# A reordered second tile list, and gathers of two sequences moved ahead of three scatters on GpSimd

## What is computed

```python
x = x + 0.5 * ffn(layernorm(x))      # 12 experts, 3 per token, hidden size 512, exact gelu
x = x + attn(layernorm(x))           # gates, convolution along the sequence, norm, gated dense layers
x = x + 0.5 * ffn(layernorm(x))
```

## Time and profile before

| what | us |
|---|---|
| median of 3 runs | 615.02 (612.63 to 616.59) |
| the profiled execution's own time | 614.01 |
| its span, first to last instruction | 612.3 |
| PE busy in it | 559.2 |
| POOL busy in it | 403.8 |

### The profile page before, as it was taken

How to read it: one execution, slowest core, us unless ns; L and a number is a source line. 1 busy time by engine, 2 the same in 40 slices (tenths; PEclk the granted TensorE clock), 3 DMA queues, 4 the chain that set the end, 5 groups by cost and what they waited for, 6 DMA issues and landing times.

```text
span 612.3 us, 17470 instructions
## 1 busy us (share of the span) xinstructions
PE 559.2 (91%) x4625; PEld 523.3 (85%) x4625; DVE 369.6 (60%) x1735; ACT 514.3 (84%) x1462; POOL 403.8 (66%) x424
## 2 busy tenths in 40 slices
PE   6899887999999999989899798998799799999996
PEld 6789887999999888868799697877699799999992
DVE  7977899441111586988775578997727632232225
ACT  4547994799989989889988699988689789989885
POOL 1076577777746777137677777767777777777771
PEclk9789999899999999999999799999999999999999
DMA  7997243243463434112355333232254532433264
GB/s 197 316 234 212 54 135 88 79 131 104 123 180 101 123 87 118 52 48 71 91 160 136 87 88 98 83 107 67 67 148 111 139 89 72 117 90 85 64 232 138
DMA packets 99127, 72.28 MB, mean 118 GB/s; under 512 B 13520, under 2 KB 91910, under 8 KB 99033
## 3 DMA queue, kind: packets, MB, share of 16 engines
q1 hardware_dynamic: 83032, 43.62, 25.7%
q0 software_dynamic: 13024, 26.11, 15.0%
q10 hardware_dynamic: 2976, 1.44, 0.8%
HBM read 37.08 MB, written 34.75 MB: 117 GB/s over the span
## 4 chain that ended last, share of the span: by engine, by line
PE 32%; DVE 21%; POOL 17%; issue 12%; ACT 8%; DMA 7%; ACTq 1%; DVEq 1%; POOLq 0%; SPq 0%
PE ps L1017 12%; PE ps L1032 12%; POOL YG L822 10%; DMA YG<-ys,SY 4%; POOL xs L806 4%; ACT hT L1205 3%; POOL yk L832 3%; DVE YG L1717 2%; DMA yk<-Ys,row 2%; PE ps L1007 2%; DVE st L1274 2%; DVE Ys L2059 1%; DVE X L1330 1%; PE ps L987 1%; DVE X L1316 1%
## 5 line engine op out<-in xcount | busy, mean ns | idle before, releaser
L1205 ACT ACTIVATE hT<-ps,BU 128x128 f32<-128x128 f32 x900 | 261.5, 392 | 43.9 <-PE ps L1017 34.5
L1017 PE MATMUL ps<-xT,WT 128*128 128x128 f32 x1800 | 243.1, 279 | 8.6 <-ACT hT L1205 5.5
L1032 PE MATMUL ps<-WD,hT 128*128 x1800 | 240.9, 277 | 6.8 <-DVE Ys L2059 6.8
L1017 PEld LDWEIGHTS ps<-xT,WT 128*128 128x128 f32 x1800 | 222.9, 194 | 18.2 <-issue 16.4
L1032 PEld LDWEIGHTS ps<-WD,hT 128*128 128x128 f32 x1800 | 221.4, 194 | 8.4 <-issue 8.3
L806 POOL DMA_INDIRECT xs<-XN,SX x144 | 142.4, 989 | 70.7 <-issue 63.3
L822 POOL DMA_INDIRECT YG<-ys,SY x132 | 130.6, 990 | 49.3 <-issue 35.4
L1088 ACT ACTIVATE WT<-WU 128x512 f32 x225 | 150.2, 668 | 7.5 <-DVE eW L1750 3.3
L2059 DVE TENSOR_TENSOR Ys<-ps,BD 128x128 f32<-128x128 f32 x225 | 54.8, 285 | 146.5 <-PE ps L1032 140.4
L832 POOL DMA_INDIRECT yk<-Ys,row x71 | 70.7, 995 | 21.9 <-issue 12.2
L793 POOL DMA_INDIRECT xl<-xna,SG x24 | 23.1, 961 | 37.4 <-DMA xna<-XN 27.6
(11 more groups left out here) (366 smaller groups left out, 592.2 us busy)
## 6 DMA issues: line engine op xcount, KB each, us to landing
ys<-Ys SPq DMA_DIRECT2D x41, 256.0 KB
xl<-xs SPq DMA_DIRECT2D x94, 64.0 KB
xl<-xs SPq DMA_DIRECT2D x71, 66.0 KB
WU<-in_L_ffn_Wup_dram SPq DMA_DIRECT2D x12, 256.0 KB, 4.6
WD<-in_L_ffn_Wdown_dram SPq DMA_DIRECT2D x12, 256.0 KB, 4.7
YG<-yk SPq DMA_DIRECT2D x4, 768.0 KB, 6.2
xs<-XN,SX POOLq DMA_INDIRECT x144
YG<-ys,SY POOLq DMA_INDIRECT x132
```

Source lines behind the costliest of these rows:

```text
L1017: x = e.matmul(HB[i % 2][:, c * P:(c + 1) * P], WT[i % NW][:, c, :], xT[m % 2][:, j * P:(j + 1) * P], start=True, stop=True)
L1032: x = e.matmul(YB[u % 2][:, j * D:(j + 1) * D], hT[i % 3][:, c * P:(c + 1) * P], WDf[:, bass.ds(r + c * P, P)], start=(c == 0), stop=(c == ...
L1205: x = e.activation(hT[i % 3][:, c * P:(c + 1) * P], HB[i % 2][:, c * P:(c + 1) * P], ACT.Gelu, bias=BU[:, bass.ds(b + c, 1)])
```

## The change

`FRONT[1]` goes from 3 to 2 and the front of list 1 from 12 to 24 tiles: these now hold every tile, begun or full, that has rows of sequences 4 and 5, filled up with other tiles of the list. Since begun tiles also hold rows of later sequences, the first load of list 1 waits for the scatters of all four sequences. POOL gathers sequences 4 and 5 after the first 24 tiles of list 1 are stored, and does so before it scatters sequences 0 to 2 for list 2.

```diff
-FRONT = (HS, 3, 2, 3)
-GA = tuple(-((E * (P - 1) - (K * (AT[1] * (n == 1) + 4 * f) - FULL * (n == 1)) * P) // P) // 4 for n, f in enumerate(FRONT))
+FRONT = (HS, 2, 2, 3)
+GA = tuple((K * (AT[1] + 4 * f) + E - FULL) // 4 if n == 1 else -((E * (P - 1) - K * 4 * f * P) // P) // 4
+           for n, f in enumerate(FRONT))
...
-POOL = (("Y", 0), ("Y", 1), ("Y", 2), ("Y", 3), ("K", 0), ("K", 1), ("K", 2), ("Y", 4), ("Y", 5), ("Y", 6), ("Y", 7),
+POOL = (("Y", 0), ("Y", 1), ("Y", 2), ("Y", 3), ("Y", 4), ("Y", 5), ("K", 0), ("K", 1), ("K", 2), ("Y", 6), ("Y", 7),
         ("K", 3), ("K", 4), ("K", 5), ("K", 6), ("K", 7))
...
                 if g == 0:
-                    for w in scattered(n, FRONT[n]):
+                    for w in scattered(n, FRONT[n] if n > 1 else len(SEQS[n])):
                         e.wait_ge(*w)
...
                 if t == 0 and k == 0:
                     e.wait_ge(s_sy, n + 1)
-                    for m in range(GROUP0[n + 1] - NYS, GROUP0[n + 1]):
+                if k == 0 and (t == 0 or n == 1 and t == 4 * FRONT[1]):
+
+                    done = GROUP0[1] + GA[1] if n == 1 and t == 0 else GROUP0[n + 1]
+                    for m in range(done - NYS, done):
                         for w in stored(m):
                             e.wait_ge(*w)
...
-                    dv.on(e.scalar_tensor_tensor(c7[:], part, -float(P - 1), c4[:], ALU.add, ALU.add))
+                    dv.on(e.tensor_tensor(c7[:], part, c4[:], ALU.add))
...
+                    dv.on(e.tensor_tensor(remX[:], nte[:], donW[:], ALU.subtract))
...
+                    dv.on(e.tensor_tensor_scan(rem[:], one[:], remX[:], 0.0, ALU.mult, ALU.add))
...
-                    dv.on(e.tensor_tensor(rem[:], endW[:], remW[:], ALU.subtract))
-                    dv.on(e.tensor_tensor(basW[:], endW[:], donW[:], ALU.subtract))
+                    dv.on(e.tensor_tensor(rem[:], rem[:], remX[:], ALU.subtract))
+                    e.wait_ge(s_dv, dv.n)
+                    dv.on(e.tensor_scalar(rem[:], rem[:], endW[:, E:EX], None, ALU.add))
                     e.wait_ge(s_dv, dv.n)
                     dv.on(e.tensor_scalar(rem[:], rem[:], -1.0, float(NTL[0] + NA[1]), ALU.mult, ALU.add))
+                    e.wait_ge(s_dv, dv.n)
+                    dv.on(e.scalar_tensor_tensor(remX[:], rem[:], 0.0, remX[:], ALU.max, ALU.min))
+                    e.wait_ge(s_dv, dv.n)
+                    dv.on(e.tensor_tensor(remW[:], remW[:], remX[:], ALU.add))
+                    dv.on(e.tensor_tensor(don4[:], donW[:], remX[:], ALU.add))
+                    e.wait_ge(s_dv, dv.n - 1)
+                    dv.on(e.tensor_tensor_scan(endW[:], one[:], remW[:], 0.0, ALU.mult, ALU.add))
+                    e.wait_ge(s_dv, dv.n)
+                    dv.on(e.tensor_scalar(endW[:], endW[:], endC[:, E:EX], None, ALU.add))
...
-                    dv.on(e.scalar_tensor_tensor(don4[:], rem[:], 0.0, remW[:], ALU.max, ALU.min))
-                    e.wait_ge(s_dv, dv.n)
-                    dv.on(e.tensor_tensor(don4[:], don4[:], donC[:], ALU.add))
-                    e.wait_ge(s_dv, dv.n)
                     dv.on(e.tensor_tensor(rem[:], nte[:], don4[:], ALU.subtract))
```

More of the change, by code:

```diff
@@ L428, in macaron_kernel @@
             "wB", "remB", "endB", "basB", "don1", "don2", "donC", "remC", "endC", "basC", "endR", "basR"))
-        donW, remW, endW, basW, don4 = (sb(n, [P, EX]) for n in ("donW", "remW", "endW", "basW", "don4"))
+        donW, remW, endW, basW, don4, remX = (sb(n, [P, EX]) for n in ("donW", "remW", "endW", "basW", "don4", "remX"))
         nt6, remL, endL, basL, dltL, stpL, c6 = donC, remC, endC, basC, basB, step3, mixed
@@ L822, in gather_y @@
                 e.indirect_dma_start(
-                    YG[:, (AT[n] + t) % 16, k, :], None, ys[n],
+                    YG[:, (AT[n] + t) % 16, k, :], None, ys[n][0:(NTL[0] - NM + NA[1]) * P] if n == 1 and t < 4 * FRONT[1] else ys[n],
                     bass.IndirectOffsetOnAxis(SY[n][:, t // 4, k, t % 4:t % 4 + 1], 0)).then_inc(s_air[j % AIR], 16)
@@ L1901, in second @@
                     dv.on(e.tensor_tensor(remW[:], donW[:], donC[:], ALU.subtract))
-                    e.wait_ge(s_dv, dv.n)
+                    dv.on(e.tensor_tensor(remX[:], nte[:], donW[:], ALU.subtract))
+                    e.wait_ge(s_dv, dv.n - 2)
                     dv.on(e.tensor_tensor_scan(endC[:], one[:], remC[:], float(NM), ALU.mult, ALU.add))
+                    e.wait_ge(s_dv, dv.n - 2)
                     dv.on(e.tensor_tensor_scan(endW[:], one[:], remW[:], 0.0, ALU.mult, ALU.add))
-                    e.wait_ge(s_dv, dv.n)
+                    e.wait_ge(s_dv, dv.n - 2)
+                    dv.on(e.tensor_tensor_scan(rem[:], one[:], remX[:], 0.0, ALU.mult, ALU.add))
+                    e.wait_ge(s_dv, dv.n - 1)
                     dv.on(e.tensor_scalar(endW[:], endW[:], endC[:, E:EX], None, ALU.add))
@@ L1909, in second @@
                     dv.on(e.tensor_scalar(lim3[:], donC[:, 0:E], float(P), None, ALU.mult))
-                    e.wait_ge(s_dv, dv.n - 2)
-                    dv.on(e.tensor_tensor(rem[:], endW[:], remW[:], ALU.subtract))
-                    dv.on(e.tensor_tensor(basW[:], endW[:], donW[:], ALU.subtract))
+                    e.wait_ge(s_dv, dv.n - 4)
+                    dv.on(e.tensor_tensor(rem[:], rem[:], remX[:], ALU.subtract))
+                    e.wait_ge(s_dv, dv.n)
+                    dv.on(e.tensor_scalar(rem[:], rem[:], endW[:, E:EX], None, ALU.add))
                     e.wait_ge(s_dv, dv.n)
                     dv.on(e.tensor_scalar(rem[:], rem[:], -1.0, float(NTL[0] + NA[1]), ALU.mult, ALU.add))
-                    dv.on(e.tensor_tensor(step3[:], basC[:, 0:E], basW[:, 0:E], ALU.subtract))
-                    dv.on(e.tensor_tensor(step2[:], basB[:, 0:E], basC[:, 0:E], ALU.subtract))
-                    e.wait_ge(s_dv, dv.n - 2)
-                    dv.on(e.scalar_tensor_tensor(don4[:], rem[:], 0.0, remW[:], ALU.max, ALU.min))
-                    e.wait_ge(s_dv, dv.n)
-                    dv.on(e.tensor_tensor(don4[:], don4[:], donC[:], ALU.add))
-                    e.wait_ge(s_dv, dv.n)
+                    e.wait_ge(s_dv, dv.n)
[3 more added lines that the diff above has]
+                    dv.on(e.tensor_tensor(don4[:], donW[:], remX[:], ALU.add))
+                    e.wait_ge(s_dv, dv.n - 1)
+                    dv.on(e.tensor_tensor_scan(endW[:], one[:], remW[:], 0.0, ALU.mult, ALU.add))
+                    e.wait_ge(s_dv, dv.n)
+                    dv.on(e.tensor_scalar(endW[:], endW[:], endC[:, E:EX], None, ALU.add))
+                    dv.on(e.tensor_tensor(step2[:], basB[:, 0:E], basC[:, 0:E], ALU.subtract))
+                    e.wait_ge(s_dv, dv.n - 1)
+                    dv.on(e.tensor_tensor(basW[:], endW[:], don4[:], ALU.subtract))
+                    e.wait_ge(s_dv, dv.n)
+                    dv.on(e.tensor_tensor(step3[:], basC[:, 0:E], basW[:, 0:E], ALU.subtract))
                     dv.on(e.tensor_tensor(rem[:], nte[:], don4[:], ALU.subtract))
```

## The result

The changed kernel takes 622.66 us (median of 4 runs, 622.22 to 623.54) where the kernel before, beside it on the same chip, took 613.83: a ratio of 1.0142 with a 95% interval of 1.0097 to 1.0187. A second series gave 623.54 against 613.56, 1.0145 (1.0121 to 1.0169). So it is slower by 1.4%, some 8.8 us. The forecast was 619.4 in a range of 610 to 627: the time lies in the range, the sign is right, but the shift is 8.8 us where +5.4 was summed. Of the two outcomes that the forecast held about equally likely, within 1% (0.47) and slower by more (0.46), the second came.

The account below looks back on a forecast made before the run. PE, busy 559.2 of 612.3 us, was taken to bound the kernel, its end hanging on POOL. The terms +2.2 + 7.1 + 2.3 - 6.2 made +5.4 us on 614.0: 619.4, range 610.0 to 627.

Parts of the forecast that it names:

- Part 1: DVE's longer table in `Q4`: list 0 ends up to 1.0 us later, bounds 0.5 to 1.3.
- part 2: List 1's first load waits for all four scatters: PE 2.2 us late, bounds 1.0 to 4.7, no half clock charged.
- part 3: 24 gathers ahead of the scatters delay list 2's first load: +7.1 us of waiting and +2.3 for half clock.
- What comes back: Ahead of `A1` of sequence 4: wait falls from 4.68 to 1.3 us, half clock goes; -6.2, bounds -3.4 and -7.5.
- The end: POOL's end follows its first scatter of sequence 6, expected near 435 us.
- The load of list 2 is not late: Rival: list 2's first load comes in time, so the change wins: 610.0 us; chance 0.12.
- Gathers slowed by DVE: Rival: half of the 24 early gathers slowed, POOL and list 2 9.2 us later: 628.6 us; chance 0.11.
- The wait before `A1` stays: Rival: sequence 4's wait has another reason than the gather, 6.2 us don't come back: 625.6 us; chance 0.13.
- The gathers are not free to go: Rival: the store of the first 24 tiles is late and holds sequence 4's gathers: some 625 us; chance 0.04.
- Slower by over 1%: Outcome: the changed kernel takes more than 620.2 us; chance 0.46.

Follow-up runs that it names:

- experiment 1: The kernel before with one edit: list 1's first load waits for all four sequences' scatters; table, tile order and GpSimd's order stay. 620.13 us, 1.0097.
- section 6: Runs pricing the half clock; over several profiles, PE's shift growth at list 1's start was 2.2 to 2.4 us with half clock, 0.6 at full clock.
- experiment 5: Four gathers fill POOL's 5.28 us hole, so scatters end earlier: only sequence 4's gathers ahead 609.26 us; control in the kernel before 613.19; in the changed kernel 617.46.
- experiment 6: The kernel before with 40 transposes that nothing reads in PE's wait ahead of `A1` of sequence 4: 612.12 us, 0.9960.
- experiment 3: The changed kernel with only sequence 4's gathers ahead of the scatters; sequence 5's go after sequence 2's scatters: 615.20 us, 1.0009.
- experiment 4: The changed kernel with 26 and 46 transposes that nothing reads in PE's waits for the first tiles of lists 1 and 2: 622.20 us, 1.0132.
- experiment 2: The changed kernel with GpSimd's order of before, scatters of sequences 0 to 2 ahead of sequence 4's gathers: 619.48 us, 1.0082.

## Why the prediction was right in kind and short by 3.4 us

**Part 1, `Q4`.** Bounded at 0.5 to 1.3 us and put inside part 2. In the changed kernel's profile tile 24 of list 0 starts at 107.06 instead of 106.19, and two tiles later nothing of that is left (112.78 against 112.75), since the half-clock stretch there also ended earlier, at 110.49 instead of 111.36. So it did not shorten PE's wait at list 1's start. But the term is smaller than what list 0's end varies by: from 1.0 us earlier to 1.8 later than in the profile of the kernel before, the latest in experiment 1, which has the old `Q4`. That the cover was missing in this profile can be chance.

**Part 2, the step that failed.** "+2.2" for list 1's first load, with "PE then idles for about 1.2 us" and "I charge none" for the clock. Measured +5.7 in the profile at list 1's second tile, +6.0 alone in the times of experiment 1. The sum by its own steps: POOL's last scatter ended at 177.56 instead of 176.83 (+0.7); the load went out 1.58 us later, where 1.56 was taken; from there to PE it was 2.07, where the landing of `wgate` gave 1.7. That makes PE 3.3 us late, 1.1 more than predicted. The cover of 1.0 us from part 1 wasn't there, so nearly all of it was idle time: 3.14 us. Behind that came 3.41 us at half clock, and the shift grew to 5.7 by the second tile; that, 2.4 us, was charged at nothing, of which 1.6 to 1.8 are the clock's (section 6). By the prediction's own reading, half clock after a wait of 2.83 us, an idle time of 3.14 would have been charged: the idle time of 1.2 was wrong first, and the clock with it. That PE would follow POOL's last scatter was in the sum. What it did not say is that POOL has no pause from 75 us up to that scatter, so that the stall can be taken away far upstream, as experiment 5 did. The Trainium skill, in "DMA: Bandwidth & Descriptors" under "Anatomy of one DMA — SWDGE (gpsimd) path", gives a DMA from GpSimd a fixed cost of about 2.0 us, most of it the wait for the write's receipt. The trace is near it, a little above: 2.55 us from the start of the last scatter to the issue of the load that waits for it (176.59 to 179.14).

**A step that no part had.** Another 1.25 us came at `A1` of sequence 0. In this profile its gathers were issued 5.73 us later than before (191.97), as much as PE was late, and `G2` got its rows 6.92 later; DVE before and after:

```profile
203.89 1.66 DVE L1330 SCALAR_TENSOR_TENSOR X<-YG,WK,X 128x128 f32<-128x128 f32 x6 [3.50 <-DMA YG<-ys,SY]
```

```profile
210.81 1.44 DVE L1334 SCALAR_TENSOR_TENSOR X<-YG,WK,X 128x128 f32<-128x128 f32 x5 [4.59 <-DMA YG<-ys,SY]
```

It is not the first load's: experiment 1 has that load's wait without the step, and the two reordered kernels of experiment 5, which have no stall at list 1's start, have the step (2.0 and 0.9 us from slot 14 to slot 15). Together the errors are +3.5 in part 2, +1.25 here, -1.0 in part 3 and -0.3 at the end, which make the 3.4 us.

**Part 3.** "+7.1" and "+2.3" for clock, 9.4 together; measured 8.4. The overfilled hole is as described: 24 gathers took 29.8 us (253.87 to 283.65; 31.0 was taken), the scatters end at 314.26 (312.1), the load goes out 1.55 us later. PE waited only 5.23 of the predicted 7 to 8 us: it came 4.8 us later than the sum had it, and the tile only 2.5 later (317.88 for 315.4). The half-clock stretch, 10.24 us with 7.48 us of work in it, was longer than the 5.66 and 3.42 it was taken from. By terms, 5.23 less the 0.63 that the prediction counted as saved is 4.6 where 7.1 was said, and half of 7.48 is 3.7 where 2.3 was said: one too large, one too small, so that the sum of the two came out near is in part luck.

**What comes back.** "-6.2" is -6.2 us: 15.37 to 9.18 between slots 48 and 61. The wait left is 1.25 (1.3 said), and no half clock follows it. For the clock's part, 2.8 us in the sum, experiment 6 measured 2.5.

**The end.** "POOL's end follows its first scatter of sequence 6": that came 8.42 us later, and the last issue 8.87 later. "Near 435" was 438.41, by the missing 3.4 us.

**The rivals.** *The load of list 2 is not late* was wrong, by 5.23 us of waiting; experiment 3 shows where it would have held, with 12 gathers. *Gathers slowed by DVE* was wrong: the 24 early gathers took at most 1062 ns each, though DVE was busy for 26.72 of the 29.78 us from 253.87 to 283.65. Nothing in these 24 calls for the Trainium skill's rule in "SBUF — State Buffer" under "SBUF: two separate sides", which stood beside this rival; whether it made the one of 1450 ns ahead of them no run here tells. *The wait before `A1` stays* was wrong (1.25 us). *The gathers are not free to go* was wrong: POOL went on after 0.30 us (253.87).

**The chances.** "Slower by over 1%" was put at 0.46, but the terms named for it, nearly all of the last three rivals' 0.28 and 0.4 of the forecast's 0.60, come to nearly 0.52, above "within 1%".

**Open.** Why the wait ahead of `A1` of sequence 0 is 1.9 to 3.3 us in eight of the nine profiles with the new order of tiles that show it (1.41 in the ninth) and 1.1 to 1.5 in the four with the old order. In the changed kernel's first profile the gathers were issued no later against PE than before, and landed later; in experiment 4 they were issued 1.4 us later against PE and landed no later. What delays them wasn't found, nor whether it is the order of tiles by itself.

## What to carry to other kernels

Before giving a load one more thing to wait for, follow that thing's engine back: if it works without a pause, the wait puts its whole backlog on the path, and a small edit far upstream can take the stall away (here four DMAs moved into a hole of 5 us won 5.3 us, with the wait left where it was). Fill a hole in an in-order queue only as far as it goes: 12 gathers fitted and brought all the gain, 24 overfilled it, and list 2's late load cost 8.4 us where 6.2 were won. And price a new idle stretch of TensorE together with the half clock that followed stretches like it in the same kernel's trace.

## What the runs showed of the hardware that was not expected

The length of a wait did not settle whether half clock follows. After 2.24 us of waiting at list 1's start PE's clock fell to 1.2 GHz in experiment 2 (its `up` at 181.71 took 1.92 us); after 2.31 us at the same place it stayed at 2.4 GHz in experiment 3 (182 to 186 us at 1.00). The changed kernel itself did both ahead of `A1` of sequence 0: full clock after 2.50 us of waiting in its first profile, half clock from 216.46 to 219.87 us after 2.27 in its second. And in experiment 3 PE's clock fell around 302 to 306 us, where no wait of more than 1.0 us stands ahead of it in the 12 us before; the same wait of 1.0 us stands there in the changed kernel's profile, and its clock stayed up. Transposes that nothing reads kept it at 2.4 GHz in every wait that they filled; where they ended 2.48 us early, they did not.
